# Last tile of every second edge block fetched row by row by SyncE instead of by a GpSimd gather, in a graph layer on one Trainium2 core

## What is computed

```python
h = jnp.maximum(_layernorm(x, axis=-1), 0.0)           # 12500 x 128
row, col = (edge_index[0], edge_index[1])              # src, dst: 400000 each
m_in = jnp.concatenate([h[row], edge_attr], axis=1)    # edge_attr: 400000 x 64
m = jax.nn.relu(m_in @ msg_w1 + msg_b1)
messages = m @ msg_w2 + msg_b2
aggregated = jax.ops.segment_sum(messages, col, num_segments=12500)
u_in = jnp.concatenate([h, aggregated], axis=1)
u = jax.nn.relu(u_in @ upd_w1 + upd_b1)
out = x + u @ upd_w2 + upd_b2
```

## Time and profile before

| | us |
|---|---|
| median of 3 runs (3936.56 to 3939.78) | 3937.84 |
| the profiled execution, whole | 3936.85 |
| its span, first to last instruction | 3935.0 |
| GpSimd busy in it | 2952.3 (75%) |
| TensorE busy in it | 2438.7 (62%) |
| VectorE busy in it | 1449.3 (37%) |
| ScalarE busy in it | 537.6 (14%) |

### The profile page before, as it was taken

The page is one execution under the profiler, slowest core; times in us unless marked ns, Lnnn a source line. Parts: engine busy times, 40 slices in busy tenths (PEclk is TensorE's granted clock), DMA queues, the critical chain, the costliest instruction groups (busy, mean ns, idle before and its releaser), DMA issues.

```text
span 3935.0 us, 32488 instructions
## 1 busy us (share of the span) xinstructions
PE 2438.7 (62%) x10672; PEld 2096.1 (53%) x10672; DVE 1449.3 (37%) x1593; ACT 537.6 (14%) x629; POOL 2952.3 (75%) x3133
## 2 busy tenths in 40 slices
PE   6596656565666566666656665665666665666565
PEld 4585555554555555555545555555555555555555
DVE  6673333333333333333333333333333333344433
ACT  6321111011111101111110111111111111111111
POOL 7777777777777777777777777777777777777776
PEclk9797777767776777777777766777776777777776
DMA  8232222223222222222222222222222222343322
GB/s 229 86 104 84 78 81 81 77 77 85 77 77 80 81 77 77 85 76 77 79 84 77 77 85 77 77 77 85 77 77 85 77 77 77 100 114 108 111 82 71
DMA packets 154626, 340.77 MB, mean 87 GB/s; under 512 B 73896, under 2 KB 74920, under 8 KB 154188
## 3 DMA queue, kind: packets, MB, share of 16 engines
q0 software_dynamic: 100000, 205.00, 19.9%
q1 hardware_dynamic: 46165, 121.97, 9.8%
q10 hardware_dynamic: 8406, 13.14, 1.0%
HBM read 327.06 MB, written 12.81 MB: 86 GB/s over the span
## 4 chain that ended last, share of the span: by engine, by line
POOL 52%; issue 21%; PE 14%; DMA 6%; DVE 4%; ACT 1%; ACTq 0%; POOLq 0%; SPq 0%; DVEq 0%
POOL rows L392 26%; POOL x_all L392 26%; PE pre L475 7%; PE seg L521 4%; DMA x_all<-table,index 2%; DMA rows<-table,index 2%; DVE rows L965 1%; DVE x_all L965 1%; DMA x_all<-in_x 1%; PE spare L569 1%; ACT rows L740 1%; DVE space L1005 1%; PE pre L496 1%; PE pre L505 0%; PE spare L536 0%
## 5 line engine op out<-in xcount | busy, mean ns | idle before, releaser
L475 PE MATMUL pre<-w_attr_sb,attrs 128*128 128x256 f32 x3126 | 1347.8, 604 | 1370.0 <-DVE rows L965 684.7
L392 POOL DMA_INDIRECT x_all<-table,index x1536 | 1449.1, 943 | 468.1 <-issue 457.4
L392 POOL DMA_INDIRECT rows<-table,index x1517 | 1434.0, 945 | 472.1 <-issue 451.4
L475 PEld LDWEIGHTS pre<-w_attr_sb,attrs 128*128 128x128 f32 x3126 | 908.8, 306 | 1607.3 <-DVE rows L965 702.3
L965 DVE TENSOR_TENSOR x_all<-pre,x_all 128x1024 f32<-128x1024 f32 x192 | 234.9, 1224 | 1134.0 <-DMA x_all<-table,index 1127.0
L965 DVE TENSOR_TENSOR rows<-pre,rows 128x1024 f32<-128x1024 f32 (+1 forms) x190 | 232.1, 1222 | 1100.7 <-DMA rows<-table,index 1095.9
L521 PEld LDWEIGHTS seg<-space,rows 128*128 128x128 f32 x3178 | 472.3, 227 | 27.8 <-ACT rows L728 5.2
L521 PEld LDWEIGHTS seg<-space,x_all 128*128 128x128 f32 x3072 | 462.6, 229 | 23.0
L521 PE MATMUL seg<-space,rows 128*128 128x80 f32 x3178 | 450.2, 304 | 5.0 <-ACT rows L728 4.8
L1019 DVE TENSOR_REDUCE h_space<-space 128x240 f32<-128x1920 f32 x130 | 440.8, 3390 | 0.0
L521 PE MATMUL seg<-space,x_all 128*128 128x80 f32 x3072 | 438.5, 306 | 0.0
(11 more groups left out here) (80 smaller groups left out, 529.3 us busy)
## 6 DMA issues: line engine op xcount, KB each, us to landing
attrs<-in_attr SPq DMA_DIRECT2D x130, 768.0 KB
x_all<-table,index POOLq DMA_INDIRECT x1536, 2.5
rows<-table,index POOLq DMA_INDIRECT x1517, 2.5
table<-rows SPq DMA_DIRECT2D x25, 224.0 KB
h_space<-in_x ACTq DMA_DIRECT2D x13, 224.0 KB
out<-h_space ACTq DMA_DIRECT2D x13, 224.0 KB
x_all<-in_x ACTq DMA_DIRECT2D x12, 224.0 KB
out<-x_all ACTq DMA_DIRECT2D x12, 224.0 KB
```

The costliest lines, as they stand in the source:

```text
L392: pool.indirect_dma_start(slot_rows(j)[:, t, :], None, source, bass.IndirectOffsetOnAxis(index[0:EDGES, j, t:t + 1], 0))\
L475: return pe.matmul(columns(j, q, PAIR)[:, two * 2 * D:(two + 1) * 2 * D], attrs[:, j % 2, start:start + EDGES], w_attr_sb[:, :], start=Tru ...
```

## The change

SP fetches the last tile (tile 23, the last of group q = 2) of the blocks with odd number from 9 to 129, which are 61 blocks. GpSimd's gather for it is dropped. SP fetches the 128 rows of such a tile one by one, each with its own DMA of one row of 512 bytes out of `table`, at an address from a register. The row numbers come from SBUF (`index_rows`, a new input that is loaded once): one load fills 8 registers, and 8 DMAs follow. A tile takes two visits of SP: on the visit of block b - 3 the first 64 rows are fetched, on that of block b - 2 the other 64. So every visit from that of block 6 to that of block 127 fetches 64 rows, behind the attribute load of its own block: 122 visits, 7808 row DMAs, 976 register loads. VectorE's sum of that group waits for 7 gathers and, on a new semaphore `rows_landed[j]`, for the 128 row DMAs. SP also waits for `table` to be stored before block 0. The code for ACT in the diff is empty (`BY_ACT = ()`).

```diff
+BY_SP = (1, 3, 5, 7)
+BY_ACT = ()
+BATCH = 8
+BATCHES = P // BATCH
...
+        index_rows = sb("index_rows", [BATCHES, src_rows.shape[1]], I32)
...
+        def gathers(i, j, q):
+
+            return tiles_of(block_of(i, j), q) - (1 if q == PAIRS - 1 and single(i, j) else 0)
...
+        def fetch_rows(engine, i, j, slots, part, parts):
+
+            positions = 4 if len(slots) == 2 else 2
+            for s in slots:
+                for k in range(positions):
+                    if (s - 2 - k) % SLOTS != j:
+                        continue
+                    round_of = i + 1 if s - 2 - k < 0 else i
...
+                    each = BATCHES // positions
+                    first = (positions - 1 - k) * each
+                    for n in range(first + part * each // parts, first + (part + 1) * each // parts):
+                        if n == first:
+
+                            engine.wait_ge(hidden_summed, (target - SLOTS) * PAIRS + PAIRS)
+                        site = next(fetches)
+                        registers = [engine.alloc_register(f"row{m}_of_fetch{site}") for m in range(BATCH)]
+                        engine.load(registers, index_rows[n:n + 1, bass.ds(column, BATCH)])
+                        for m in range(BATCH):
+                            p = n * BATCH + m
+                            row = bass.RuntimeValue.of_register_unchecked(registers[m], min_val=0, max_val=N - 1)
+                            engine.dma_start(slot_rows(s)[p:p + 1, TILES_B - 1, :], table[bass.ds(row, 1), :]).then_inc(rows_landed[s], 16)
...
                 load_attr(i, j)
-
+                if BY_SP:
+                    fetch_rows(sp, i, j, BY_SP, 0, 1)
...
-                    gather(table, j, range(q * PAIR, q * PAIR + tiles_of(b, q)))
+                    gather(table, j, range(q * PAIR, q * PAIR + gathers(i, j, q)))
...
-                    dve.wait_ge(gathered[j][q], i * (16 * PAIR) + 16 * tiles)
+                    dve.wait_ge(gathered[j][q], landings(i, j, q))
+                    if q == PAIRS - 1 and single(i, j):
+                        dve.wait_ge(rows_landed[j], i * (16 * P))
```

More of the change, by code:

```diff
@@ L36, in after, with gnn_layer @@
     return step + (CREDIT + 1 - back)
-def gnn_layer(nc, x, src, src_last, dst_rows, dst_cols, attr, attr_last, w_src, w_attr, b_msg1, w_msg2_t, b_msg2, w_node, w_agg, b_upd1,
+def gnn_layer(nc, x, src, src_last, src_rows, dst_rows, dst_cols, attr, attr_last, w_src, w_attr, b_msg1, w_msg2_t, b_msg2, w_node, w_agg, b_upd1,
               w_upd2, b_upd2, out):
@@ L233, in gnn_layer @@
         index_next_loaded = sem("index_next_loaded")
+        index_rows_loaded = sem("index_rows_loaded")
+        rows_landed = [sem(f"rows_landed{j}") for j in range(SLOTS)]
         index_early_loaded = sem("index_early_loaded")
@@ L285, in ahead, with single, landings @@
             return (i, j + blocks) if j + blocks < SLOTS else (i + 1, j + blocks - SLOTS)
+        def single(i, j):
+            b = block_of(i, j)
+            return j in BY_SP + BY_ACT and (not isinstance(i, int) or i >= 1) and (not isinstance(b, int) or b < LAST)
+        def landings(i, j, q):
+            full = 16 * PAIR
+            if q < PAIRS - 1 or j not in BY_SP + BY_ACT or (isinstance(i, int) and i == 0):
+                return i * full + 16 * tiles_of(block_of(i, j), q)
+            return full + i * (full - 16)
+        def gathers(i, j, q):
+            return tiles_of(block_of(i, j), q) - (1 if q == PAIRS - 1 and single(i, j) else 0)
+        fetches = itertools.count()
+        def fetch_rows(engine, i, j, slots, part, parts):
[5 more added lines that the diff above has]
+                    round_of = i + 1 if s - 2 - k < 0 else i
+                    if not single(round_of, s):
+                        continue
+                    target = block_of(round_of, s)
+                    column = (round_of * len(BY_SP + BY_ACT) + (sorted(BY_SP + BY_ACT).index(s) - len(BY_SP + BY_ACT))) * BATCH
+                    each = BATCHES // positions
[10 more added lines that the diff above has]
+                            engine.dma_start(slot_rows(s)[p:p + 1, TILES_B - 1, :], table[bass.ds(row, 1), :]).then_inc(rows_landed[s], 16)
         def behind(i, j, blocks):
@@ L320, in _ @@
                 sp.dma_start(tile, source).then_inc(w_late_loaded, 16)
+            sp.dma_start(index_rows[:, :], src_rows).then_inc(index_rows_loaded, 16)
             def load_index(i, j):
@@ L368, in load_block @@
                 load_attr(i, j)
+                if BY_SP:
+                    fetch_rows(sp, i, j, BY_SP, 0, 1)
+            sp.wait_ge(index_rows_loaded, 16)
+            for k in range(UNROLL):
+                sp.wait_ge(table_stored[k], 16 * len(CUT) * GBODIES)
             sp.wait_ge(update_ready, after(GROUPS - 1))
@@ L755, in relu_block @@
                     relu_hidden(i, j, q)
+                    if BY_ACT:
+                        fetch_rows(act, i, j, BY_ACT, q, PAIRS)
+            if BY_ACT:
+                act.wait_ge(index_rows_loaded, 16)
+                for k in range(UNROLL):
+                    act.wait_ge(table_stored[k], 16 * len(CUT) * GBODIES)
             for j in range(EARLY, SLOTS):
@@ L1230 @@
     width = attr.shape[2]
+    fetched = [b for b in range(SLOTS, blocks) if b % SLOTS in BY_SP + BY_ACT]
+    edges = np.concatenate([np.arange(EDGES) + (b * TILES_B + TILES_B - 1) * EDGES for b in fetched])
     arrays = {
         "x": x,
+        "src_rows": src[edges].reshape(len(fetched), BATCHES, BATCH).transpose(1, 0, 2).reshape(BATCHES, -1),
         "src": src[:body].reshape(blocks, TILES_B, EDGES).transpose(0, 2, 1), "src_last": src[body:].reshape(-1, EDGES).T,
```

## The result

The changed kernel takes 4634.36 us (median of 4 runs, 4633.19 to 4635.54) against 3937.38 before: 1.177 times as long, 95% interval 1.1755 to 1.1785. The forecast was 6250 us, range 4850 to 6800.

What follows compares the result with a forecast made beforehand. GpSimd's gather issue bounds the kernel; after the change SP's own work would. Block 6's load at 247.70 us, 104 visits of 48.8 and 18 of 47.7 (5934 us), and 69 us of tail gave 6250 us, range 4850 to 6800.

Steps and rivals of the forecast that it cites:

- What bounds, what is taken away: Edge stage goes at GpSimd's gather issue, 1.248 us each; dropping 61 gathers takes away 76.1 us.
- Who waits for it: Next attribute load queues behind SP's 64 rows, so TensorE waits; SP never waits, its 48.8 us visit is the period.
- (1) The row DMA: SP's issue of one row with address work: 0.50 us, 32.0 us per visit; lower bound 0.37 us, 23.7 per visit.
- the sum: SP's visit in the loop: 32.0 us of rows, 15.5 of register loads, 1.3 of the two old loads, 48.8 together.
- (2) The register load: SP's load of eight registers: 1.82 us, 15.5 us per visit in the loop with address and gaps; bounds 2.5 to 17.
- Rival (a): SP binds, but register loads cost 0.3 to 0.75 us whatever their number: 37.3 us a visit, 4869 us; chance 0.17.
- The tail: From block 128's attribute load to the end: 26 us, then 43 for block 129, last tiles and nodes; 69 us.
- block 128 at TensorE's pace: Near the end, landing of the attributes and block 128 at the pace of TensorE: 26 us.
- (b): SP keeps up with visits under 29.33 us and GpSimd stays the bound; 3861 us, faster; chance 0.07.
- (c): Row transfers bind, not their issue, all meeting on one DMA engine; 10,200 us at 1 us a row; chance 0.12.

Runs made afterwards that it cites:

- the kernel of disputed prices: Not the layer: only copies x and issues register loads and register-address DMAs of several counts, nothing else running; SP row DMAs measured 0.218 us (1 row), 0.333 (128).

## Why the forecast was right in kind and wrong in size

**What bounds, what is taken away: right.** 76 us for 61 gathers is what came out where SP had room (3861.37 with one load a visit, 3863.52 with the rows shared between SP and ACT and the longer lead).

**Who waits for it: right for SP, TensorE and GpSimd.** From the visit of block 7 on SP never waits for more than 0.4 us; the attribute load queued behind the rows is what TensorE waits for; GpSimd waits for sums. Only VectorE's waits for gathers came otherwise, since GpSimd may be 3 groups ahead and can't fill its slots. The block 6 load went out at 244.6 us and block 128's at 4545.4, so 122 visits took 4301 us, 35.25 each.

**(1) The row DMA: the first term that was mis-sized.** The forecast took 0.50 us from the table stores and argued that the length of a DMA doesn't follow its size. That is nearly true of bytes, and of 13, 16 and 128 rows (0.311 to 0.333 in the kernel of disputed prices), but one row needs only 0.225 of SP. The other pieces, address and gaps, were right (0.18 us). Measured 0.42 on average, 27.1 us a visit where the sum had 32.0: 4.9 too much. Its stated lower bound, 0.37, held.

**(2) The register load: the larger error, and the step on which the forecast failed.** 1.82 us came from a straight line through loads of one and three registers on VectorE. Measured 0.70 on SP; with address and gaps 6.7 us a visit where the sum had 15.5, so 8.8 us too much. Rival (a), loads at a price that hardly depends on the number, was the nearer picture of these loads, and its 4869 us the nearer time, in part by luck: its rows were 4.9 us too dear and its loads, 4.0 us a visit, 2.7 too cheap. The figure of the Trainium skill, Runtime: NRT & Kernel Launch, section "Instruction fetch mechanics", about 200 ns a register even in bulk, is near VectorE's load of three (0.248 us a register) and far from the loads that the change makes, 0.087 us a register.

The two errors are 13.7 us of the 13.4 by which 48.8 missed the 35.4 of an average visit in the loop. What goes the other way is the end of each round of eight visits, which the sum didn't have: 2.6 us more between the last row and the next index load, 0.3 a visit.

**The tail: 17 us too short.** 86.3 us from block 128's attributes to the end against 69. The step "block 128 at TensorE's pace" took gathers as already made. With `LEAD = 3` they can't be; with 9 the time falls by 20 us, and 66.1 us are left behind block 128's attributes.

**The range.** The forecast named lower bounds for both unknown prices, 0.37 for a row and 0.32 for a load, but the low end of the range is (a), with the load moved and the row left at 0.50. Both errors went the same way. With both at what was measured the sum is 27.1 + 6.7 + 1.3 = 35.1 us a visit, and 247.7 + 122 x 35.1 + 71 = 4601 us: inside what the stated bounds allow, outside the range that was given.

**Rivals.** Of the signs named beforehand, that of (a) is the nearest, a period of 37 us with loads under 0.8, though the loads do grow with the number. (b) needed rows under 0.40 with loads at 0.32; the rows came within 0.02 of that, the loads, 0.83 with gaps, did not. (c) has its premise, since a row goes in one packet and so over one engine, but not its price: the same 7808 row DMAs on SP and ACT end at 3863.52 us with the longer lead, where 3861 would be the whole gain.

## What to carry to other kernels

Work that is moved to an idle queue is free until that queue's own issue time reaches the period, and then everything queued behind it is late by the whole excess; so count instructions per period, address instructions and register loads with them, and move only what fits (32 rows a visit gained 1%, 64 lost 18%). A price read off an instruction of another shape or count is an estimate that needs bounds; when two such prices make up a sum, move both together for the ends of the range. And look at how far a producer may run ahead: a lead of 3 groups cost nothing before, and 41 us as soon as the start of the loop was disturbed.

## What the runs showed of the hardware beyond that

- An SP DMA instruction with its address from a register takes 0.218 us for one row and 0.333 for 128, with 0.468 for 64 rows standing out; four times the bytes in one row add 0.01.
- A load of two registers on SP (0.640) costs more than one of four (0.470), and a load of three on VectorE (0.744) more than one of eight (0.595).
- On one chip the kernel before took 4717.45 us. In the trace of its version with a lead of 9 groups (4721.27 us there) the gathers were as long as ever (0.947 us), but between instructions of TensorE stood gaps of up to 4 us that no wait explains:

```profile
PEld seg L521 <- issue: 1626.7, 1254, 3.9
```

  There the four kernels came to 1.0007 (the kernel before with a lead of 9), 1.119 (rows on SP and ACT), 1.201 (48 rows on SP) and 1.309 times (both) the time of the kernel before on the same chip, though three of them are faster elsewhere. In the kernel with 48 rows, SP's row DMAs had lengths from 0.001 to 1.4 us:

```profile
L338 SPq DMA_DIRECT2D x_all<-table x3840: 1/228/1401, 603.9 to 5525.7; - x192
```

  What was the matter with that chip was not found; the kernels lost more with 48 rows in a visit of SP than with 32, and most with ACT's rows on top of the 48.
